# A graph network's edge step on one Trainium2 core: the destination-row products of the next group move from ahead of its source rows to right behind the current group's state products

## The chip, the core and the metric

The kernel runs on 1 core of a Trainium2 chip. The core's engines work side by side, each through its own queue of instructions in order: PE (TensorE) multiplies matrices, ACT (ScalarE) applies functions, DVE (VectorE) does elementwise work, POOL (GpSimd) here issues indirect DMAs that gather rows, SP (SyncE) issues all other DMAs. They meet through semaphores: an instruction increments one when it ends, another waits until it has a value. The metric is the device time of one execution in microseconds (us).

## The reference

Four rounds of message passing over 3125 nodes and 50,000 edges, sorted by destination. The state of a node has 128 numbers, that of an edge too.

```
edge_attr = swish(edge_attr_raw @ enc_W + enc_b)
for _ in range(4):
    e_in = concatenate([edge_attr, x[src], x[dst]])
    e_upd = layernorm(swish(e_in @ eW1 + eb1) @ eW2 + eb2) * eg + ebeta
    edge_attr = edge_attr + e_upd
    agg = segment_sum(edge_attr, dst)
    x = x + layernorm(swish(concatenate([x, agg]) @ nW1 + nb1) @ nW2 + nb2) * ng + nbeta
out = layernorm(x0 + x)
```

The hidden layer of an edge is a sum of three products: one of the edge's own state, one of its source node, one of its destination node. The kernel makes the two node products once a round for all nodes, as tables (`p_table` for sources, `q_table` for destinations), and only looks rows up per edge.

## The kernel before, in words

Each round (a *step*, `s` from 0 to 3) runs over 98 groups `g` of 512 edges (4 tiles of 128), and then over the nodes in 5 chunks, which also writes the tables for the next step. All of a step is written out flat, with no loop on the chip. On PE, `fast_pe` (line 1192) sets the order of a step, and the four parts that it calls are made by `pe_parts` (line 1088):

- `turn(g + 2)`, line 1103: 8 transposes that bring the edge state of the group after next into the form that its products need. It waits for the state's DMA (`st`) and for ACT's copy of the transposes before (`eT`).
- `hidden(g)`: three sets of products that add up in one PSUM tile `ps_h(g % 2)`. Line 1123: 4 *destination-row* products of 256 columns, which place the rows of `q_table` on edges by a 0/1 matrix; they wait for that window and matrix (semaphore `q`), and for DVE to have read the PSUM tile's last content (`hl` of group g - 2). Line 1131: 16 *source-row* products of 128 columns, which add the gathered rows of `p_table`; they wait for POOL's gathers (`rows`), and the last one signals `src`. Line 1139: 6 *state* products of 512 columns; they wait for `eT`, and signal `h`.
- `output(g - 1)`, lines 1150 and 1155: the second layer of the group before, a bias product and 24 products of 128 columns, into `ps_v`. It waits for `hl`, and signals `v`.
- `node_sums(g - 7)`, line 1171: 8 products that sum an older group's edges by destination. It signals `sum`.

So the order on PE was, for each g: rows of q (1123), source rows (1131), state (1139), transposes (1103), output (1150, 1155), sums (1171), then again with g + 1.

The other engines in a group: POOL issues 4 gathers (line 1080) for group g + 4 into the buffer that the source rows of g leave, so it waits for `src` of g. ACT makes swish of the hidden layer (lines 1242, 1243; waits for `h`), copies the transposes (1269), squares the output (1257; waits for `v`), and casts (1283). DVE makes the low half of the hidden layer (1349, signals `hl`), adds an older group's sum to `agg` (1419; waits for `sum`), finishes the norm (284 to 292, 1385, 1396, 1404), and reads the output (1359). SP issues the loads of group g + 3 (1022, 1030, 1036) and the loads and stores of older groups (1045, 1049).

The buffers for gathered rows are four deep, those for hidden and output PSUM two deep.

## Time and profile before

| what | value |
|---|---|
| median of 3 runs | 3248.82 us (3248.39 to 3252.28) |
| span of the profiled execution | 3309.1 us |
| PE busy | 2595.5 us, 78% |
| DVE busy | 2336.3 us, 71% |
| ACT busy | 2083.8 us, 63% |
| POOL busy | 1702.6 us, 51% |
| granted TensorE clock, mean | 0.947 |
| DMA | 578.05 MB, mean 175 GB/s |

The profile is of one execution, whose span from the first to the last instruction is 3309.1 us; what lies around that span isn't in it. That span is 60.3 us above the median of the runs, so a sum made on it is carried over as a ratio. "Busy" counts the time in which an engine has an instruction in work. A row of the timeline gives start, length, engine, line and operation, the tile written and the tile read, how many such instructions were merged (x16), and in brackets the engine's idle time ahead of it with what ended that. "issue" there means that the profile shows no wait, "remote" that it can't name who ended it.

### The profile page before, as it was taken

How to read it: one execution, taken by the hardware profiler on the slowest of the kernel's cores; microseconds unless marked ns; L12 is line 12 of the kernel's file. 1: busy time of each engine (PE TensorE's matmuls, PEld its weight loads, DVE VectorE, ACT ScalarE, POOL GpSimd, SP SyncE). 2: the span in 40 equal slices, each digit the busy share in tenths (PEclk: the TensorE clock that was granted, in tenths of full speed). 3: DMA queues.
4: the chain of work that ended last, by engine and by line, in shares of the span. 5: the costliest groups of instructions: out<-in, count | busy, mean ns of one | idle time of the engine just before them, and what ended most of it. 6: DMA issues, size and time to landing. Idle time of an engine off the chain costs nothing.

```text
span 3309.1 us, 86038 instructions
## 1 busy us (share of the span) xinstructions
PE 2595.5 (78%) x28086; PEld 1911.6 (58%) x28086; DVE 2336.3 (71%) x6778; ACT 2083.8 (63%) x5559; POOL 1702.6 (51%) x1679
## 2 busy tenths in 40 slices
PE   3665888888887788888887788888888688888886
PEld 1332666666664566666665566666665466666664
DVE  6884677777784577777786477777776377777777
ACT  3774666666663566666664566666675466666674
POOL 2445566566531556665640666665540665666550
PEclk8656999999999899999999899999999899999998
DMA  4776566666644566666653566666663455555550
GB/s 129 249 248 205 171 196 194 195 200 195 194 149 134 159 194 195 202 196 194 198 166 121 155 198 199 196 195 201 194 182 111 146 158 156 163 156 161 159 149 25
DMA packets 492918, 578.05 MB, mean 175 GB/s; under 512 B 82399, under 2 KB 341724, under 8 KB 492446
## 3 DMA queue, kind: packets, MB, share of 16 engines
q1 hardware_dynamic: 417198, 366.82, 34.8%
q0 software_dynamic: 75264, 205.62, 23.0%
q8 instruction: 228, 3.74, 0.5%
q14 instruction: 228, 1.87, 0.2%
HBM read 428.62 MB, written 144.35 MB: 173 GB/s over the span
## 4 chain that ended last, share of the span: by engine, by line
PE 59%; issue 16%; ACT 6%; DVE 6%; another core or an unknown queue 6%; DMA 3%; SPq 1%; DVEq 1%; POOL 0%; ACTq 0%; POOLq 0%
PE psum L1155 13%; PE psum L1139 13%; PE psum L1131 12%; PE psum L1123 5%; PE psum L1103 5%; PE psum L1171 4%; PE psum L1150 2%; PE psum L1577 2%; PE psum L1616 2%; ACT arena L1269 1%; ACT psum L1243 1%; ACT arena L1257 1%; PE psum L1590 1%; DMA arena<-attr_p 1%
## 5 line engine op out<-in xcount | busy, mean ns | idle before, releaser
L1080 POOL DMA_INDIRECT arena<-node_tables,idx_all x1568 | 1582.0, 1009 | 1342.0 <-PE psum L1131 626.5
L1257 ACT ACTIVATE arena<-psum 128x128 f32<-128x128 f32 x1568 | 411.6, 278 | 741.3 <-remote 723.1
L1131 PE MATMUL psum<-ident,arena 128*128 128x128 f16 x6272 | 548.1, 220 | 410.6 <-issue 398.8
L1131 PEld LDWEIGHTS psum<-ident,arena 128*128 128x128 f16 x6272 | 399.3, 98 | 541.1 <-issue 521.9
L1349 DVE SCALAR_TENSOR_TENSOR arena<-psum,arena 128x1024 f16<-128x1024 f32 x392 | 477.0, 1217 | 202.9 <-issue 146.9
L1155 PE MATMUL psum<-w_hi,arena 128*128 128x128 f16 x6272 | 595.2, 220 | 4.6 <-DVE arena L1349 3.5
L1155 PE MATMUL psum<-w_lo,arena 128*128 128x128 f16 x3136 | 550.5, 220 | 1.2 <-issue 1.2
L1419 DVE TENSOR_TENSOR agg<-agg,psum 128x128 f32 x392 | 113.0, 288 | 569.5 <-remote 544.8
L1242 ACT ACTIVATE arena<-psum 128x1024 f16<-128x1024 f32 x392 | 402.2, 1026 | 172.3 <-remote 75.7
L1155 PEld LDWEIGHTS psum<-w_hi,arena 128*128 128x128 f16 x6272 | 502.2, 98 | 6.8 <-DVE arena L1349 4.7
L1139 PE MATMUL psum<-arena,w_hi 128*128 128x512 f16 x1568 | 479.7, 386 | 29.8 <-issue 29.6
L1385 DVE SCALAR_TENSOR_TENSOR arena<-arena 128x128 f32<-128x128 f32 x1568 | 489.9, 346 | 4.0 <-DVE arena L288 0.4
L1269 ACT COPY arena<-psum 128x1024 f16<-128x1024 f16 x392 | 400.0, 1020 | 45.7 <-remote 22.0
L1243 ACT ACTIVATE psum<-psum 128x1024 f32<-128x1024 f32 x392 | 401.2, 1023 | 0.0
L1155 PEld LDWEIGHTS psum<-w_lo,arena 128*128 128x128 f16 x3136 | 308.8, 98 | 48.3 <-issue 3.5
L1257 ACT ACTIVATION_READ_ACCUMULATOR arena<-psum 128x1 f32 x1568 | 325.8, 208 | 0.0
L1139 PE MATMUL psum<-arena,w_lo 128*128 128x512 f16 x784 | 303.1, 387 | 7.8 <-issue 7.6
L1103 PEld LDWEIGHTS psum<-ident,arena 128*128 128x128 f16 x3136 | 211.5, 100 | 144.1 <-issue 46.6
L1359 DVE TENSOR_TENSOR arena<-psum,g_row 128x512 f32<-128x512 f32 x392 | 266.3, 679 | 30.3 <-ACT arena L1257 27.5
L1396 DVE SCALAR_TENSOR_TENSOR arena<-arena 128x512 f32<-128x512 f32 x392 | 279.2, 712 | 6.7
L1123 PE MATMUL psum<-arena 128*128 128x256 fp8e4 x1568 | 253.0, 274 | 36.3 <-issue 23.2
L1103 PE MATMUL psum<-ident,arena 128*128 128x128 f16 x3136 | 245.5, 222 | 41.4 <-DMA arena<-state 18.2
(172 smaller groups left out, 3514.9 us busy)
## 6 DMA issues: line engine op xcount, KB each, us to landing
state<-arena SPq DMA_DIRECT2D x392, 256.0 KB, 3.8
arena<-state SPq DMA_DIRECT2D x392, 256.0 KB
arena<-matrices SPq DMA_DIRECT2D x784, 64.0 KB
arena<-node_tables SPq DMA_DIRECT2D x784, 64.0 KB
node_tables<-arena SPq DMA_DIRECT2D x100, 256.0 KB, 2.4
arena<-node_tables,idx_all POOLq DMA_INDIRECT x1568
arena<-rel_rows SPq DMA_DIRECT2D x98, 128.0 KB, 3.9
matrices<-arena SPq DMA_DIRECT2D x98, 128.0 KB, 3.6
```

Of the source, the lines that this page charges most:

```text
L1080: pool.indirect_dma_start(out=rows[k][:, t, :], out_offset=None, in_=p_table, in_offset=bass.IndirectOffsetOnAxis(ap=idx_all[:, g, t:t + 1 ...
L1103: x = pe.transpose(ps_t[:, n * P:(n + 1) * P], st_in[k8][:, t, p * D:(p + 1) * D], ident16[:, :])
L1123: pe.matmul(ps_h(k2)[:, half, :].rearrange("q (t p) -> q t p", t=TPG)[:, :, h * HALF_N:(h + 1) * HALF_N], q_win[k][:, h * H + half * D:h * ...
L1131: x = pe.matmul(ps_h(k2)[:, half, t * P:(t + 1) * P], rows[k][:, t, p * H + half * D:p * H + half * D + D], ident16[:, :], start=False, st ...
L1139: x = pe.matmul(ps_h(k2)[:, half, :], w[:, cols], eT[k2][:, p, :], start=False, stop=w is w1_lo, skip_group_check=True)
L1155: x = pe.matmul(ps_v(k2)[:, t * P:(t + 1) * P], h[k2][:, half, t * P:(t + 1) * P], w[:, half, :], start=False, stop=half == 1 and h is hl, ...
L1242: act.activation(hh[k2], ps_h(k2), ACT.Silu).then_inc(S("hh"), 1)
L1243: act.activation(ps_h(k2), ps_h(k2), ACT.Silu).then_inc(S("h32"), 1)
L1257: x = act.activation(sq[k2][:, t * P:(t + 1) * P], ps_v(k2)[:, t * P:(t + 1) * P], ACT.Square, accum_out=nv[pair][:, n:n + 1])
L1269: act.copy(eT[k2].rearrange("p k e -> p (k e)"), ps_t[:, :]).then_inc(S("eT"), 1)
L1349: dve.scalar_tensor_tensor(hl[k2], ps_h(k2), 1.0, hh[k2], ALU.mult, ALU.subtract).then_inc(S("hl"), 1)
L1385: x = dve.scalar_tensor_tensor(e_new[k][:, t * P:(t + 1) * P], gu[k][:, t * P:(t + 1) * P], rs[pair][:, n:n + 1], st_in[k8][:, t, D:2 * D] ...
```

## The change

The 4 destination-row products of a group (line 1123, with their waits for `q` and `hl`) become a part of their own, `targets`. In a step's order it stands ahead of the loop for group 0, and in the loop right behind `hidden(g)` for group g + 1; before, it was the first piece of `hidden(g + 1)`, behind `node_sums(g - 7)`. No product is added, removed or changed, and no other engine's order is changed. The body of the general path (`pe`, for other inputs) keeps its order.

```diff
-                def hidden(i, off):
+                def targets(i, off):
                     if not self.has(i, off):
                         return
...
+                def hidden(i, off):
+
+                    if not self.has(i, off):
+                        return
+                    k, k2 = off % R, off % 2
                     pe.wait_ge(*self.gathered_dyn(s, i, off))
...
             def fast_pe(self, pe, s, node):
...
                 turn(0, 0)
                 turn(0, 1)
+                targets(0, 0)
                 for g in range(G1):
                     hidden(0, g)
+                    targets(0, g + 1)
                     turn(0, g + 2)
                     output(0, g - 1)
                     node_sums(0, g - LAG - 3)
```

The lines behind it shift by six: line 1131 is 1137 afterwards, 1139 is 1145, 1150 is 1156, 1155 is 1161, 1171 is 1177; 1103 and 1123 keep their numbers.

The order on PE in the middle of a step before, from the last output product of one group to the transposes of the next (the names in brackets are the semaphores waited for; `edge_oh` is the matrix of the sums, `edge_rows` the gathers, `edge_st` the state):

```order
L1155 MATMUL psum<-w_hi,arena 128x128
L1171 MATMUL psum<-arena 128x128 [waits edge_oh2,edge_el,edge_added]
L1171 MATMUL psum<-arena 128x128 x7
L1123 MATMUL psum<-arena 128x4x64 [waits edge_q2,edge_hl]
L1123 MATMUL psum<-arena 128x4x64 x3
L1131 MATMUL psum<-ident,arena 128x128 [waits edge_rows2]
L1131 MATMUL psum<-ident,arena 128x128 x15
L1139 MATMUL psum<-arena,w_hi 128x512 [waits edge_eT]
L1139 MATMUL psum<-arena,w_hi 128x512
L1139 MATMUL psum<-arena,w_lo 128x512
L1139 MATMUL psum<-arena,w_hi 128x512 x2
L1139 MATMUL psum<-arena,w_lo 128x512
```

The same stretch on PE now:

```order
L1161 MATMUL psum<-w_hi,arena 128x128
L1177 MATMUL psum<-arena 128x128 [waits edge_oh2,edge_el,edge_added]
L1177 MATMUL psum<-arena 128x128 x7
L1137 MATMUL psum<-ident,arena 128x128 [waits edge_rows2]
L1137 MATMUL psum<-ident,arena 128x128 x15
L1145 MATMUL psum<-arena,w_hi 128x512 [waits edge_eT]
L1145 MATMUL psum<-arena,w_hi 128x512
L1145 MATMUL psum<-arena,w_lo 128x512
L1145 MATMUL psum<-arena,w_hi 128x512 x2
L1145 MATMUL psum<-arena,w_lo 128x512
L1123 MATMUL psum<-arena 128x4x64 [waits edge_q3,edge_hl]
L1123 MATMUL psum<-arena 128x4x64 x3
```

The source rows now follow the sums directly, and the destination-row products of the group after stand behind the state products, ahead of the transposes, the output and the sums.

At the start of a step, on PE, the second group's place before:

```order
L1139 MATMUL psum<-arena,w_lo 128x512
L1103 MATMUL psum<-ident,arena 128x128 [waits edge_eT,edge_st2]
L1103 MATMUL psum<-ident,arena 128x128 x7
L1123 MATMUL psum<-arena 128x4x64 [waits edge_q1]
L1123 MATMUL psum<-arena 128x4x64 x3
L1131 MATMUL psum<-ident,arena 128x128 [waits edge_rows1]
```

And now:

```order
L1145 MATMUL psum<-arena,w_lo 128x512
L1123 MATMUL psum<-arena 128x4x64 [waits edge_q1]
L1123 MATMUL psum<-arena 128x4x64 x3
L1103 MATMUL psum<-ident,arena 128x128 [waits edge_eT,edge_st2]
L1103 MATMUL psum<-ident,arena 128x128 x7
L1137 MATMUL psum<-ident,arena 128x128 [waits edge_rows1]
```

There the wait for the second group's window (`edge_q1`) has moved ahead of the third group's transposes.

## Rows read from the trace of the kernel before

**Rows 1.** Waits over the whole span: who waited for whom, us in total, times, longest.

```profile
ACT arena L1257 <- remote: 723.1, 353, 3.2
POOL arena L1080 <- PE psum L1131: 626.5, 361, 3.6
...
PE psum L1131 <- issue: 398.8, 769, 1.9
```

**Rows 2.** Windows of two steps, gathers (line 1080) alone: us, POOL busy, (xcount).

```profile
409.00:935.00 526.00, 315.65 (x313) 1.00 0.67 197
...
2677.00:3180.00 503.00, 305.06 (x302) 1.00 0.55 158
```

**Rows 3.** The chain that ended last, 1500 to 1514 us: start, us, what.

```profile
1503.59 0.45 PE psum L1171 x8
1504.03 0.44 PE psum L1123 x4
```

**Rows 4.** Timeline of one group in mid-step: start, us, engine, line, count, [idle before].

```profile
1500.56 1.20 POOL L1080 DMA_INDIRECT arena<-node_tables,idx_all  x1 [1.94 <-PE psum L1131]
...
1503.31 0.95 POOL L1080 DMA_INDIRECT arena<-node_tables,idx_all  x1 [0.30 <-issue]
...
1503.37 0.22 PE L1155 MATMUL psum<-w_hi,arena 128*128 128x128 f16 x1
...
1504.31 0.33 PE L1131 MATMUL psum<-ident,arena 128*128 128x128 f16 x3
...
1504.92 0.33 PE L1131 MATMUL psum<-ident,arena 128*128 128x128 f16 x3 [0.28 <-issue]
...
1506.42 0.67 PE L1131 MATMUL psum<-ident,arena 128*128 128x128 f16 x9 [0.53 <-issue]
1506.54 0.28 ACT L1257 ACTIVATE arena<-psum 128x128 f32<-128x128 f32 x1 [2.04 <-remote]
...
1507.36 0.94 POOL L1080 DMA_INDIRECT arena<-node_tables,idx_all  x1 [1.85 <-PE psum L1131]
```

**Rows 5.** Timeline of a group whose output products end early against the gathers.

```profile
487.39 0.94 POOL L1080 DMA_INDIRECT arena<-node_tables,idx_all  x1 [1.06 <-PE psum L1131]
...
488.90 0.22 PE L1155 MATMUL psum<-w_hi,arena 128*128 128x128 f16 x1
...
489.84 0.74 PE L1131 MATMUL psum<-ident,arena 128*128 128x128 f16 x6
...
493.25 0.28 ACT L1257 ACTIVATE arena<-psum 128x128 f32<-128x128 f32 x1 [3.14 <-remote]
```

**Rows 6.** Timeline of a group whose output products end late against the gathers.

```profile
2186.05 0.22 PE L1155 MATMUL psum<-w_hi,arena 128*128 128x128 f16 x1
...
2186.99 0.83 PE L1131 MATMUL psum<-ident,arena 128*128 128x128 f16 x9
2188.20 0.55 PE L1131 MATMUL psum<-ident,arena 128*128 128x128 f16 x7 [0.38 <-issue]
```

**Rows 7.** Timeline of an early group of a step, which has no sums yet.

```profile
1875.19 0.22 PE L1155 MATMUL psum<-w_hi,arena 128*128 128x128 f16 x1
...
1875.68 0.94 PE L1131 MATMUL psum<-ident,arena 128*128 128x128 f16 x14
```

**Rows 8.** Timeline of two groups in a row, the first without a stop in its source rows.

```profile
1379.84 1.35 POOL L1080 DMA_INDIRECT arena<-node_tables,idx_all  x1 [1.63 <-PE psum L1131]
...
1383.58 1.06 PE L1131 MATMUL psum<-ident,arena 128*128 128x128 f16 x16
...
1386.32 0.94 POOL L1080 DMA_INDIRECT arena<-node_tables,idx_all  x1 [1.38 <-PE psum L1131]
...
1393.04 1.34 POOL L1080 DMA_INDIRECT arena<-node_tables,idx_all  x1 [1.55 <-PE psum L1131]
```

**Rows 9.** Timeline of the group of rows 4: DVE's low half, SP's window load.

```profile
1503.66 1.23 DVE L1349 SCALAR_TENSOR_TENSOR arena<-psum,arena 128x1024 f16<-128x1024 f32 x1 [0.27 <-issue]
...
1506.36 0.95 SPq L1036 DMA_DIRECT2D arena<-node_tables  x2
```

More of the change, by code:

```diff
@@ L1173, in node_sums @@
                     x.then_inc(S("sum"), 1)
-                return turn, hidden, output, node_sums
+                return turn, targets, hidden, output, node_sums
             def pe(self, pe, s):
-                turn, hidden, output, node_sums = self.pe_parts(pe, s)
+                turn, targets, hidden, output, node_sums = self.pe_parts(pe, s)
                 turn(0, self.lo)
@@ L1183, in body @@
                     for j in range(self.U):
+                        targets(i, j)
                         hidden(i, j)
@@ L1192, in fast_pe @@
             def fast_pe(self, pe, s, node):
-                turn, hidden, output, node_sums = self.pe_parts(pe, s)
+                turn, targets, hidden, output, node_sums = self.pe_parts(pe, s)
                 node_hidden, node_output, node_tables_of = node.pe_parts(pe, s)
```

## The prediction, made before the changed kernel ran

> **What bounds the kernel now.** I read the waits over the span first: who waits for whom, summed. Three stand out [rows 1]: ACT's square (line 1257) waits 353 times, 723 us, for an event the profile calls "remote"; POOL's gathers (1080) wait 361 times, 627 us, for the source rows (1131); and PE itself is idle 399 us ahead of source rows with "issue", which names no wait. There are 392 groups, so each happens nearly once a group. Next the windows over the gathers alone, which give the cycle: 313 gathers in 526.00 us are 6.72 us per four, 302 in 503.00 are 6.66 [rows 2]. PE's own work is less: in rows 4 it starts 7 rows between 1504.31 and 1506.42, 0.4 us of work in 2.1 us, so 1.7 us of a cycle are idle and 5.0 are work. PE's amount of work does not bound, whatever its share of busy time.
>
> The timeline of one group shows the ring [rows 4]. POOL starts its first gather at 1500.56. PE starts the last output product at 1503.37, goes through sums and targets (0.45 and 0.44 us in the chain, [rows 3]), starts source rows at 1504.31, and then stops: 3 rows, a gap, a few more, gaps of 0.28 and 0.53 us. At 1506.42 it runs free and does the last 9 rows. At 1506.54, within 0.12 us of that, ACT gets the signal `v` of the output product that had been started 3.17 us earlier, having idled 2.04 us. So products, and the signals of products already done, are held up together and come free together. What does the release follow? From the first gather to ACT's start it is 1506.54 - 1500.56 = 5.98 us here, and 493.25 - 487.39 = 5.86 where PE was early [rows 5], though from the last output product it is 3.17 against 4.35 us. The release keeps step with POOL's four gathers, not with PE. Behind it come the source rows that are left; the last signals `src`; and POOL's next first gather starts, 1507.36 here, 0.82 us behind the release.
>
> So a cycle is 5.9 us of gathers up to the release, then the rows left, then the signal. One row takes (1.06 - 0.22) / 15 = 0.056 us, from a run of 16 and the 0.22 us that one product alone shows [rows 4, 8]. Nine rows left put 8 x 0.056 = 0.45 us on the path. The floor is seen where all 16 rows were done before the release: 1386.32 - 1379.84 = 6.48 us, and the cycle behind it took 6.72 again, a mean of 6.60 for the pair [rows 8]. Only the rows left at the release can be bought, up to 6.70 - 6.48 = 0.22 us a group (6.70 the rounded mean of rows 2).
>
> **What decides how many are left.** PE stops 1.1 us after its last output product: 8 sums, 4 targets and 3 rows got started (1503.37 to 1504.47, [rows 4]). In the early group it is 8, 4 and 6, up to about 490.2 [rows 5]; in the late group 8, 4 and 9 [rows 6]. Where there are no sums, 4 targets and 14 rows got through [rows 7]. The count behind `v` is thus 15, 18, 21, and 18: it does not depend on what kinds the products are, and the group without sums has simply brought more source rows through. I read this as an allowance behind the held signal: PE may start some 15 to 21 products past `v`.
>
> **The change part by part.** It adds and removes no instruction. It takes 4 targets, 0.44 us, out of the stretch between `v` and the source rows and puts them behind the state products, ahead of transposes and output.
> - Source rows relative to `v`: 0.44 us, or 4 products, closer. With the same allowance 4 more rows start before the stop: 9 left become 5. Saved 4 x 0.056 = 0.22 us at most per group, which lands on the floor (6.48).
> - `v` itself: 0.44 us later against the source rows ahead of it. Its natural end would still be well ahead of the release: in rows 4 it is held by more than 2 us (ACT's idle time). So this costs nothing in the held groups. Cover gone, it is 0.44 us in a group.
> - `hl` wait moved ahead: targets for g + 1 need DVE's low half of g - 1. DVE ends it at 1503.66 + 1.23 = 1504.89 [rows 9]; the moved targets start behind the state products, which come behind the last row, so after 1506.42 + 8 x 0.056 = 1506.9. Margin over 2 us. Behind them on PE stand transposes, output and sums; none waits. Cost 0.
> - `q` wait moved ahead past transposes, output and sums (at most half a cycle, 3.4 us). SP loads at 1506.36 a window that is for a later group [rows 9], about three ahead: a cycle of 6.7 us or more is left. Cost 0. No DMA and no queue of SP or POOL is moved.
> - At a step's start the second group's window is now waited for ahead of the third group's transposes, 8 products of 128 columns like the rows (8 x 0.056 = 0.45 us) that no longer cover the wait: at most 4 x 0.45 = 1.8 us, at least 0. Near the end, where no gathers run, `v` comes 0.44 us later; with some four such groups a step that is 0 to 7 us in all. I take 1 us for both, since PE is ahead of the others there, and do not carry it into the sum.
>
> How much of the 0.22 us stays is the unknown. If every group is brought to the floor it is 0.22; if groups alternate as in rows 8, each short one followed by a long one, the mean is 6.60 and the gain 0.10. Less than zero is bounded by the rival below (+0.22). I take 0.12, near the alternating pair, the only row that shows a short cycle and what follows it. Groups: 353 waits of ACT [rows 1] are 88 a step; less the first eight of a step, without sums and mostly through their rows already [rows 7], 80 x 4 = 320. Sum: 320 x 0.12 = 38 us, 3309.1 - 38.4 = 3270.7 us of profiled span. As a ratio that is 0.9884, and on the median of 3248.82 it gives 3211 us. All of the 0.22 would be 70 us, ratio 0.9787, 3180 us; 0.10 gives 3217 us.
>
> **Rivals.**
> *No change, 3249 us.* The profiled span is 60.3 us above the median. Over 320 groups that is 0.19 us a group, close to the 0.22 us above the floor. If the drip of rows exists only in the profiled execution, timed runs already cycle at POOL's 6.48 and nothing is to be had; the profile after would be shorter and the runs not. For it: the size agrees, and POOL never shows a cycle under the floor. Against it: without any hold the cycle would be near PE's 5.0 us and the runs far shorter than 3249, so most of the hold is in them. The same result comes if the release follows the last rows rather than POOL, or if POOL's 0.5 us from signal to gather grows. The Trainium skill, page "NOTIFIC — the notification-queue block", section "7.1 Overflow: three behaviours, one of which stalls the engine", says that the path from engine to queue never drops a record but backpressures, so recording can hold up an engine. No row here tells a record from a signal; by that rule the profiled stops would be those of the recorder, and the time would be this rival's.
>
> *Slower, about 3318 us.* The stop may be set not by a count behind `v` but by the time since a gather began: in rows 4 the third gather starts at 1503.31 and PE stops 1.16 us later. If PE may start only so many products after that moment, the targets, which take 0.11 us each where rows take 0.056, no longer carry it through that time; source rows start 0.44 us sooner against PE's own order, but PE's whole phase is set by `src`, so the output products come 0.44 us later after it, and with them everything behind. Then the rows reached at the stop do not rise, and by the count lost, 4 rows more are left: 0.22 us x 320 = 70 us, span 3379.5, 3318 us. It decides where the moment of the third gather falls within output or sums. Against it: in rows 6 nine rows were started with the same four targets, and in rows 5 six, at another phase to the gathers; and rows 7 show count, not phase. For it: the phase between source rows and gathers is by construction nearly fixed, so the three rows do not vary it much.
>
> *Moved waits, 3250 to 3258 us.* The step's start and end cost their 1.8 and 7 us and the gain in the middle is nil.
>
> **How the numbers follow.** The forecast has 0.44 (all faster outcomes, from 3165 to 3242), no change 0.34, the slow rival 0.16, moved waits 0.06. A measurement of this kernel tells about 0.2%, 6.5 us, from no change. The likeliest gives 3211 us, its own range 3180 to 3240. The range of eight in ten takes in the unchanged case and the moved waits: 3180 to 3268. Left out is the full slow rival and what would be beyond the floor.
>
> **What the profile after would show.** Right: windows over line 1080 give 6.5 to 6.6 us per four gathers in place of 6.7; behind ACT's start at 1257 run 4 to 5 rows, not 9; PE's stop begins some 15 to 18 products after the last output product with 7 or more rows done; POOL's wait for the source rows falls by 0.1 us a gather set. Wrong: the same windows at 6.7 with as many rows left, meaning the stop is not counted from `v`; or 6.9 and more, with 12 to 13 left. A wait of PE at line 1123 of over 0.3 us in mid-step would mean that the moved `q` or `hl` wait has no margin. A shorter span with unchanged runs would speak for the first rival.

## The result, and the profile after

The changed kernel took 3257.46 us (median of 20 runs, 3251.22 to 3261.22), the kernel before 3252.07 us in the same series (median of 20, 3243.91 to 3262.22). The ratio is 1.0015, with a 95% interval of 1.0008 to 1.0022: no gain, if anything a trace slower. The forecast was 3211 us. Ratios compare executions in the faster of two states; two executions fell out of it, one of the kernel before at 7612 us and one of two_targets at 3361 us, both on chip 12.

The profiled execution of the changed kernel has a span of 3254.9 us, 2 us under its own time of 3256.65. That of the kernel before had 3309.1 us, while the slowest of its 20 runs took 3262.22 us, so the profile is of none of them. This matters for all that compares the two profiles below. The waits of the changed kernel over the whole span, in us in total, times, longest:

```profile
ACT arena L1266 <- remote: 655.9, 347, 3.2
POOL arena L1080 <- PE psum L1137: 530.8, 354, 3.7
...
PE psum L1137 <- issue: 326.2, 699, 2.7
```

These answer to [rows 1]. All three fell, by 67, 96 and 73 us. The gathers over the window of the same 526 us as in [rows 2], and over the last step (us, POOL's busy time, number of gathers):

```profile
409.00:935.00 526.00, 335.53 (x321) 0.99 0.68 202
2677.00:3180.00 503.00, 304.25 (x296) 0.99 0.55 158
```

321 in place of 313 gathers in 526 us is a cycle of 6.55 us in place of 6.72. (The second window holds 296 in place of 302: the changed kernel's last step ends 54 us earlier, and the window reaches into its tail.) Seen against [rows 4], a pair of groups shows what the forecast had in mind. Start, us, engine, line, count, idle time before:

```profile
802.86 1.43 POOL L1080 DMA_INDIRECT arena<-node_tables,idx_all  x1 [1.35 <-PE psum L1137]
...
805.85 0.94 POOL L1080 DMA_INDIRECT arena<-node_tables,idx_all  x1 [0.30 <-issue]
...
806.10 0.22 PE L1161 MATMUL psum<-w_hi,arena 128*128 128x128 f16 x1
...
806.61 1.08 PE L1137 MATMUL psum<-ident,arena 128*128 128x128 f16 x14
...
808.07 0.27 PE L1137 MATMUL psum<-ident,arena 128*128 128x128 f16 x2 [0.38 <-issue]
...
808.91 0.28 ACT L1266 ACTIVATE arena<-psum 128x128 f32<-128x128 f32 x1 [2.11 <-remote]
...
809.40 0.95 POOL L1080 DMA_INDIRECT arena<-node_tables,idx_all  x1 [1.35 <-PE psum L1137]
...
812.01 1.39 POOL L1080 DMA_INDIRECT arena<-node_tables,idx_all  x1 [0.30 <-issue]
...
812.49 0.22 PE L1161 MATMUL psum<-w_hi,arena 128*128 128x128 f16 x1
...
812.99 0.28 PE L1137 MATMUL psum<-ident,arena 128*128 128x128 f16 x2
...
813.72 0.38 PE L1137 MATMUL psum<-ident,arena 128*128 128x128 f16 x4 [0.45 <-issue]
...
814.46 0.45 PE L1137 MATMUL psum<-ident,arena 128*128 128x128 f16 x5 [0.35 <-issue]
...
815.20 0.44 PE L1137 MATMUL psum<-ident,arena 128*128 128x128 f16 x5 [0.30 <-issue]
...
815.34 0.28 ACT L1266 ACTIVATE arena<-psum 128x128 f32<-128x128 f32 x1 [2.00 <-remote]
...
815.92 1.47 POOL L1080 DMA_INDIRECT arena<-node_tables,idx_all  x1 [1.26 <-PE psum L1137]
```

The source rows now start 0.5 us behind the last output product (806.10 to 806.61), where it was 0.94 [rows 4]. But it is the output product that has moved, not the rows. From POOL's first gather to the last output product it is 806.10 - 802.86 = 3.24 us, where it was 1503.37 - 1500.56 = 2.81; from the first gather to the first source row it is 806.61 - 802.86 = 3.75 us, and it was 1504.31 - 1500.56 = 3.75. In the first group all 16 are started by 808.13, 0.8 us ahead of the release at 808.91. But POOL does not start then. It starts at 809.40, 0.49 us behind the *release*: the signal `src` is held like every other. From first gather to first gather this is 6.54 us, near the 6.48 of [rows 8]. In the next group the source rows meet the stop after 2 products, and the last 5 come with the release; its cycle is 6.52 us.

By profile against profile this looked like a success: 54 us less, where the sum had said 38. By the runs it was nothing: either the profile of before was not typical, or the change is worth less than it seems. The experiments were to tell these apart.

In what follows the same quantities were counted from each timeline over the 332 groups from the 9th to the 91st of each step. The release is taken as ACT's start on `v`. "Left" is the number of source rows that start later than 0.14 us ahead of it, since the last burst of rows begins by about that much before ACT does (1506.42 against 1506.54 in [rows 4]). "The first stop" is the first pause of over 0.33 us between the starts of two products behind the last output product.

### The profile page after: what moved, and what is told of

It is laid out like the page before. It is cut to its first block, busy times and chain, and to the rows that moved or that the text cites. A ratio compares the mean times of both kernels' runs of the same rounds, so it can differ in the third digit from the quotient of the medians.

```text
span 3254.9 us, 86038 instructions
## 1 busy us (share of the span) xinstructions
PE 2596.9 (80%) x28086; PEld 1917.8 (59%) x28086; DVE 2347.8 (72%) x6778; ACT 2081.9 (64%) x5559; POOL 1735.2 (53%) x1679
## 3 DMA queue, kind: packets, MB, share of 16 engines
q8 instruction: 228, 3.74, 0.5%
## 4 chain that ended last, share of the span: by engine, by line
PE 71%; issue 14%; DVE 5%; DMA 3%; another core or an unknown queue 3%; ACT 2%; SPq 1%; DVEq 1%; POOL 0%; ACTq 0%; POOLq 0%
PE psum L1145 16%; PE psum L1161 15%; PE psum L1137 14%; PE psum L1177 5%; PE psum L1103 5%; PE psum L1123 5%; PE psum L1156 3%; PE psum L1586 2%; DMA arena<-attr_p 2%; PE psum L1625 2%; PE psum L1599 1%; PE psum L784 1%; DVE arena L1394 1%; DVEq L885 0%
## 5 line engine op out<-in xcount | busy, mean ns | idle before, releaser
L1080 POOL DMA_INDIRECT arena<-node_tables,idx_all x1568 | 1613.4, 1029 | 1252.3 <-PE psum L1137 530.8
L1137 PE MATMUL psum<-ident,arena 128*128 128x128 f16 x6272 | 542.3, 220 | 336.3 <-issue 326.2
L1137 PEld LDWEIGHTS psum<-ident,arena 128*128 128x128 f16 x6272 | 386.6, 98 | 449.5 <-issue 435.8
L1145 PE MATMUL psum<-arena,w_hi 128*128 128x512 f16 x1568 | 488.0, 390 | 36.2 <-issue 35.5
L1177 PE MATMUL psum<-arena 128*128 128x128 fp8e4 x3136 | 248.2, 219 | 26.8 <-issue 21.1
L1413 DVE SCALAR_TENSOR_TENSOR arena<-arena 128x512 f16<-128x512 f32 x392 | 268.6, 685 | 0.2
L1123 PE MATMUL psum<-arena 128*128 128x256 fp8e4 x1568 | 245.1, 279 | 29.3 <-issue 16.5
```

The costliest lines, as they stand in the source:

```text
L1080: pool.indirect_dma_start(out=rows[k][:, t, :], out_offset=None, in_=p_table, in_offset=bass.IndirectOffsetOnAxis(ap=idx_all[:, g, t:t + 1 ...
L1123: pe.matmul(ps_h(k2)[:, half, :].rearrange("q (t p) -> q t p", t=TPG)[:, :, h * HALF_N:(h + 1) * HALF_N], q_win[k][:, h * H + half * D:h * ...
L1137: x = pe.matmul(ps_h(k2)[:, half, t * P:(t + 1) * P], rows[k][:, t, p * H + half * D:p * H + half * D + D], ident16[:, :], start=False, st ...
L1145: x = pe.matmul(ps_h(k2)[:, half, :], w[:, cols], eT[k2][:, p, :], start=False, stop=w is w1_lo, skip_group_check=True)
L1177: x = pe.matmul(ps_a[:, 0:P], st_out[k][:, t, p * D:(p + 1) * D], oh[k][:, t * P:(t + 1) * P], start=t == 0 and p == 0, stop=t == TPG - 1 ...
```

## The experiments

Six series were run, and they fall into levels. "Held" means that recorded updates of semaphores, of engines and transfers alike, grow rare from about 3 us behind POOL's first gather on (1 to 3 in each half us up to 5.5 us), and then come in a burst (12 to 20 in each half us up to 6.5; before, before_3, after, after_3). In before_again they come evenly, 14 to 18 in each half us. A series ran on one chip each, so a property of the chip can't be told from one of the series.

| series | before, median us | held |
|---|---|---|
| chip 14 | 2734 | no |
| chip 4 | 2728 | no |
| the case's own | 3252 | yes |
| chip 5 | 3259 | yes |
| chip 12 | 3308 | yes |
| chip 2 | 3309 | yes |

### Both kernels again (before_again, after_again, before_2, before_3, after_3)

No edit. What was expected of before_again:

> The kernel before, unchanged, for a second profile. What is to be told apart: the first profile of before has a span of 3309 us, 60 above its median, and a steady cycle of 6.71 us; the changed kernel's has 3255, equal to its median, and 6.56. Theory A: the first profile was an unusual execution of before; the usual one has a span near 3250, a mean steady cycle near 6.55 us and 5 or 6 source rows left at the release, so that nothing was there to be bought. Theory B: the profile of before is always some 60 us longer than the runs; then it comes out near 3309 again with 8 rows left. Ratio to before 1.000 +- 0.001.

Of after_again:

> The changed kernel again. Theory A: ratio 1.000 to 1.003, span and median within 3 us of each other, steady cycle 6.55 us as in its first profile. Theory B gives the same. If its profile now comes out at 3309 while its runs stay at 3257, both spans are possible for both kernels.

Measured on chip 14: before_again 2734.87 us, ratio 0.9994 (0.9982 to 1.0007); after_again 2729.40 us, ratio 0.9982 (0.9971 to 0.9994). Neither theory had this: the whole kernel takes 16% less there. The changed kernel is 5 us faster on that chip. The timeline of the kernel before on chip 14:

```profile
1009.68 0.38 PE L1150 MATMUL psum<-v_bias,ones 128*128 128x512 f16 x1
...
1012.04 0.95 POOL L1080 DMA_INDIRECT arena<-node_tables,idx_all  x1 [0.30 <-issue]
...
1012.12 1.06 PE L1131 MATMUL psum<-ident,arena 128*128 128x128 f16 x16
...
1012.20 0.29 ACT L1257 ACTIVATE arena<-psum 128x128 f32<-128x128 f32 x1
...
1013.29 0.95 POOL L1080 DMA_INDIRECT arena<-node_tables,idx_all  x1 [0.30 <-issue]
...
1014.75 0.38 PE L1150 MATMUL psum<-v_bias,ones 128*128 128x512 f16 x1
```

No stop in the 16 source rows, and no "remote" wait of ACT. From output to output it is 5.07 us: PE is packed here, and POOL gathers without rest, one each 1.25 us. (The mean of all groups counted is 5.29 us.) The stops and waits on which the prediction stood are not there.

> The kernel before once more. The first series ran with every semaphore update held between 2.5 and 5.3 us behind POOL's first gather (cycle 6.5 to 6.7 us, 3250 us in all); the second, on a chip numbered 14, ran the same kernels without the hold (cycle 5.07 us, 2734 us). Theory H: the hold is a property of the chip or the execution, not of the kernel; so this comes out either near 2734 or near 3250, with nothing between. If it is near 3250: theory A says its profile shows a mean steady cycle near 6.55 us and 5 or 6 rows left at the release; theory B says 6.7 us and 8 rows with a span 60 us above the median.

On chip 4: 2725.36 us, ratio 0.9998 (0.9978 to 1.0018). Not held either.

> The kernel before on whatever chip comes. Chips 14 and 4 ran it without held updates (2734 and 2728 us), the series of the case with them (3252 us). Theory H: one of the two states again, nothing between. Near 3250 it gives the missing second profile of before with held updates: mean steady cycle near 6.55 us (theory A) or near 6.7 us (theory B).

On chip 12: 3310.16 us, ratio 1.0008 (0.9995 to 1.0020), span 3301.7. This is a second profile of before with held updates, and it reads like the first: cycle 6.70 us, 7.0 rows left (the first: 6.72 and 7.9), and its waits are near those of [rows 1]:

```profile
ACT arena L1257 <- remote: 736.4, 361, 3.2
POOL arena L1080 <- PE psum L1131: 604.8, 359, 3.9
...
PE psum L1131 <- issue: 380.3, 754, 3.7
```

But on this chip the runs too are at 3308, and this profiled execution is one of them. So B falls. The first profile of before reads like an ordinary execution at the 3308 level, beside runs at the 3252 level; that it was taken on another chip is likely and not shown. Whether theory A's 6.55 us and 5 or 6 rows hold for the kernel before at the 3252 level stays open, since no profile of it was taken there.

> The changed kernel beside the kernel before on one chip more. So far three levels of before were seen: 2731 (chips 14, 4; no held updates), 3252 (the case's series) and 3308 (chip 12, held, where before's profile read like the one of rows 1 to 9: span 3302, cycle 6.69). Held updates: theory G (given back: fewer rows are left at the release, but POOL then starts late in the next group, so the mean stays near the floor of the hold) expects a ratio of 0.997 to 1.002, as targets_late had 0.997; the prediction's sum expects 0.988. Not held: 0.998.

On chip 5: 3260.76 us, ratio 1.0004 (0.9994 to 1.0013), cycle 6.58 us, 5.5 rows left. The ratio is as theory G had it; its reason is tested under targets_late. The profile of the changed kernel on chip 5 is like its first one; its time equals that of the kernel before on the same chip.

### Targets behind the transposes (targets_late)

```diff
-                    targets(0, g + 1)
                     turn(0, g + 2)
+                    targets(0, g + 1)
```

> The changed kernel with the targets of g + 1 behind the transposes of g + 2, ahead of the output. Without held updates, theory W (what the change gains there, 5 us, comes from the 0.44 us of targets that stand ahead of the transposes and cover their wait for SP's load of the state, whose sum fell from 107 to 46 us): the gain is gone, the transposes wait about 107 us again, ratio to before 0.999 to 1.001. Rival W2, the gain comes from the targets' leaving the stretch ahead of the source rows: it stays, 0.997 to 0.999. With held updates: as the changed kernel, 1.000 to 1.003, by either.

On chip 12 (held): 3299.15 us, ratio 0.9970 (0.9958 to 0.9981). For the stretch between output and source rows this is the same edit as the change, and it has the kernel before's profile beside it on the same chip. Gathers in two windows, first before_3, then targets_late:

```profile
1150.00:1650.00 500.00, 302.16 (x298) 1.00 0.67 197
2650.00:3150.00 500.00, 311.71 (x301) 1.00 0.56 160
```

```profile
1150.00:1650.00 500.00, 312.64 (x300) 0.99 0.67 198
2650.00:3150.00 500.00, 315.37 (x302) 1.00 0.56 160
```

599 against 602 gathers in 1000 us: 6.68 and 6.65 us a cycle, 0.03 us or a quarter of what the forecast took. The runs, 9.2 us faster, say 0.02 us a group. Three things were counted to see why it is so little.

First, the place of PE's work against POOL's gathers (medians, us behind POOL's first gather; the stop behind the third):

| | last output product | first source row | first stop, behind the third gather | products from the last output product to the stop |
|---|---|---|---|---|
| before | 2.81 | 3.74 | 1.20 | 15 |
| before_3 | 2.81 | 3.74 | 1.21 | 14 |
| targets_late | 3.24 | 3.74 | 1.19 | 11 |
| after | 3.24 | 3.74 | 1.17 | 11 |
| after_3 | 3.24 | 3.75 | 1.18 | 11 |

The change moves the output product 0.43 us later. The source rows start where they did, since PE's work from one group's rows to the next is the same in sum. The stop stays where it was too, against the gathers, and the products that pass behind `v` fall from 14 or 15 to 11. An allowance counted from `v` would have kept its number. Within each of these kernels it is the same: a later output product doesn't move the stop (slope -0.07 to -0.32, where a count would give 1).

Second, the parts of the cycle (means, us):

| | last row to POOL's start | POOL's start to release | release to last row | cycle | left | groups with none left |
|---|---|---|---|---|---|---|
| before_3 | 0.617 | 5.937 | 0.143 | 6.697 | 7.0 | 28 |
| targets_late | 0.772 | 5.952 | -0.046 | 6.678 | 5.7 | 62 |

The last row comes 0.19 us sooner against the release, but this is a mean in which groups that are through before the release count as negative. What stands on the path is only what runs behind the release, and that shrinks from 0.245 to 0.195 us. The first column grows for the same reason: in groups with no row left POOL starts 1.72 us behind the last row in targets_late, against 0.55 in the others, because it starts with the release.

Third, the cycle of before_3 by rows left: 6.52 us with none to 3, 6.61 with 4 to 7, 6.78 with 8 to 11. So below 4 rows nothing more is gained. At these prices the rows left in targets_late would be worth 0.05 us; measured are 0.02, since its groups with 4 to 11 left take 0.03 to 0.05 us longer than those of before_3. Theory G's reason, a long group behind each short one, is hardly there: behind a group with none left the cycle is 6.72 us in targets_late and 6.67 behind the others, which makes under 0.01 us in the mean, and in after and after_3 it is not longer at all (6.55 against 6.57, 6.57 against 6.58). One such group and the one behind it, in targets_late, a case where it was long:

```profile
841.74 1.39 POOL L1080 DMA_INDIRECT arena<-node_tables,idx_all  x1 [1.50 <-PE psum L1137]
...
845.49 1.09 PE L1137 MATMUL psum<-ident,arena 128*128 128x128 f16 x15
...
846.97 0.22 PE L1137 MATMUL psum<-ident,arena 128*128 128x128 f16 x1 [0.39 <-issue]
...
847.75 0.28 ACT L1266 ACTIVATE arena<-psum 128x128 f32<-128x128 f32 x1 [2.06 <-remote]
...
848.24 0.94 POOL L1080 DMA_INDIRECT arena<-node_tables,idx_all  x1 [1.34 <-PE psum L1137]
...
853.34 0.38 PE L1137 MATMUL psum<-ident,arena 128*128 128x128 f16 x4 [0.46 <-issue]
...
854.09 0.83 PE L1137 MATMUL psum<-ident,arena 128*128 128x128 f16 x12 [0.37 <-issue]
...
854.30 0.28 ACT L1266 ACTIVATE arena<-psum 128x128 f32<-128x128 f32 x1 [2.12 <-remote]
```

PE was through at 846.97, 0.78 us ahead of the release; POOL came at 848.24 all the same, and the group behind it had 10 rows left and started its next gathers only at 855.19.

### Half the targets (two_targets)

```diff
-                            for h in range(2):
+                            for h in range(2 if off < 2 and s == 0 else 1):
```

> The changed kernel with 2 of the 4 targets of every group but the first two left out (half the destination rows are missing). Without held updates, theory P (PE is packed, 5.07 us a group is its own work): 0.22 us x 390 = 86 us less, ratio 0.967. Rival, POOL's gathers at 4 x 1.25 = 5.0 us a group are the floor: ratio over 0.985. With held updates: no change by either, since PE is not the bound there, ratio 0.99 to 1.00.

On chip 12: 3287.32 us, ratio 0.9932 (0.9914 to 0.9951). This run starts from the changed kernel, so it is to be held against targets_late on the same chip: 0.22 us of PE work less a group, 86 us in all, gave 12 us (21 against before). So where updates are held PE's amount of work is mostly, not wholly, off the path.

### Sums ahead of the output too (sums_ahead, sums_ahead_2, sums_ahead_3)

```diff
-                    output(0, g - 1)
                     node_sums(0, g - LAG - 3)
+                    output(0, g - 1)
```

> The changed kernel with the node sums ahead of the output products too, so that the source rows follow the output directly, 0.45 us nearer to its signal. Theory 1 (gathers set a floor of about 6.45 us, and after already is within 0.1 us of it): no gain, 3240 to 3262 us, though rows left at the release fall from 5 to 1 or 2. Rival, the rows left are still what costs: 4 fewer of them give 0.2 us a group, 3190 us.

> The changed kernel with the sums ahead of the output. Where updates are held: theory A (after is within 0.1 us a group of a floor that the held updates set) gives ratio 0.995 to 1.003; the prediction's theory (4 more products off the stretch are 0.2 us a group) gives 0.98. Where they are not held: 0.995 as in the series before.

> Sums ahead of the output too. Held updates: theory G 0.995 to 1.002, with half the groups or more at 0 rows left; the prediction's mechanism, doubled, 0.976. Not held: 0.995 to 0.997, as twice before.

Measured: chip 14, 0.9949 (0.9930 to 0.9968); chip 4, 0.9971 (0.9956 to 0.9987); chip 5 (held), 0.9984 (0.9975 to 0.9993). On chip 5 it stands beside after_3:

| | last row to POOL's start | POOL's start to release | release to last row | cycle | left | groups with none left |
|---|---|---|---|---|---|---|
| after_3 | 0.699 | 5.882 | -0.004 | 6.578 | 5.5 | 64 |
| sums_ahead_3 | 1.009 | 5.889 | -0.331 | 6.567 | 3.8 | 113 |

1.7 rows fewer are left (0.09 us at 0.056 a row). The last row comes 0.33 us sooner against the release, POOL's start behind it comes 0.31 us later, and the cycle falls by 0.01. Within one chip and one series this says that fewer rows left at the release buy next to nothing here. extra_ops below says it too: 3.8 rows left, cycle 6.58. It is the best of the kernels that keep the order of the gathers, by 0.2 to 0.5% against before.

### Fewer gathers (half_gathers, half_gathers_2, half_gathers_3, three_gathers)

```diff
-                    for t in range(TPG):
+                    for t in range(2):
                         pool.indirect_dma_start(
...
-                                              rows[k][:, t, ...
+                                              rows[k][:, t % 2, ...
```

and the counts waited for with 2 in place of 4; three_gathers has 3.

> The changed kernel with 2 gathers for a group in place of 4; the source rows use each gathered tile twice (this part of the computation is changed). Theory 1, the gathers of POOL and the release behind them set the cycle (5.9 us from first gather to release, of 4 gathers): the release comes some 2.5 us sooner, PE's own 5.0 us bound, cycle 6.56 to about 5.1, time down by 1.4 x 340 = 480 us to about 2780. Rival, PE's stops have another source (its own signals, or SP's loads and stores) and POOL only follows: cycle still over 6.3 us, time over 3160.

> The changed kernel with 2 gathers for a group in place of 4 (source rows use each gathered tile twice, which changes that part of the computation). Where updates are held (before near 3250): if the hold follows the gathers, the cycle falls to about 5.1 us and the time to about 2800; if it has another source the time stays over 3150. Where they are not: 2645 us as in the series before, ratio 0.967.

> 2 gathers for a group in place of 4 (source rows use each tile twice). Held updates: if the hold comes from the gathers' work or their updates (32 of some 220 a group fewer), the cycle falls to 5.1 to 5.9 us, time under 3050; if the hold has nothing to do with them, over 3200. Not held: 2646 as before.

> The changed kernel with 3 gathers for a group in place of 4 (the fourth tile's source rows use the first's). Held updates: theory T (there is a threshold in how densely gathers come; with 3 in 5.07 us POOL rests 1.3 us and the hold goes) expects 5.1 to 5.3 us a group and a ratio of 0.82 to 0.84, as with 2. Rival R2 (each gather costs a fixed part of the hold, 1.6 us): 4.9 us, so PE's 5.07 again or a little over; rival K2, one hold for each group that ends with its last gather's landing, 1.3 us sooner: cycle 5.3 to 5.5 us, ratio 0.84 to 0.87. Not held: 0.967 to 0.975.

Not held: 0.9665 (0.9643 to 0.9686) on chip 14, 0.9706 (0.9679 to 0.9733) on chip 4. Held: 0.8191 (0.8173 to 0.8209) on chip 5, 2669 us in place of 3259. The gathers are what makes the hold; with 2 a held chip is no slower than another by more than 1%. (Their number, their bytes and POOL's time in them fall together here, and no run tells these apart.) The timeline on chip 5 with 2 gathers:

```profile
1204.22 1.01 POOL L1080 DMA_INDIRECT arena<-node_tables,idx_all  x1 [2.55 <-PE psum L1137]
...
1205.53 0.95 POOL L1080 DMA_INDIRECT arena<-node_tables,idx_all  x1 [0.30 <-issue]
...
1207.96 1.06 PE L1137 MATMUL psum<-ident,arena 128*128 128x128 f16 x16
...
1208.05 0.29 ACT L1266 ACTIVATE arena<-psum 128x128 f32<-128x128 f32 x1
...
1209.29 0.99 POOL L1080 DMA_INDIRECT arena<-node_tables,idx_all  x1 [2.81 <-PE psum L1137]
```

POOL's start comes each 5.07 us, all 16 rows pass, ACT does not wait. With three gathers, on chip 2: 0.8629 (0.8613 to 0.8644), 2857 us. Windows of 400 us on chip 2 (three) and chip 5 (two):

```profile
1000.00:1400.00 400.00, 224.03 (x215) 1.00 0.73 212
```

```profile
1000.00:1400.00 400.00, 163.33 (x150) 1.00 0.70 204
```

The first is 400 / (215 / 3) = 5.6 us a group. So held chips take 5.1, 5.6 and 6.6 us with two, three and four gathers. That is nearest to rival K2, one hold a group that ends behind the last gather: its ratio is met (0.84 to 0.87), its cycle missed by 0.1 us. That the hold ends with the last gather's landing is not shown by this.

### The gathers spread (spread_gathers)

```diff
                     for t in range(TPG):
+                        if t == 2 and g - R - 1 >= self.lo:
+                            pool.wait_ge(S("v"), s * self.per_step + g - R)
                         pool.indirect_dma_start(
```

> The changed kernel, all work kept, with POOL waiting for v of two groups back ahead of the third of a group's four gathers. With held updates (before 3250 to 3310): theory Q (the hold comes where a third and fourth gather follow the first two with no pause; half_gathers on such a chip had none) expects the hold to go and the cycle to fall from 6.58 us to what POOL then needs, about 0.5 + 2.5 + 0.8 + 2.5 - 0.7 = 5.6 us: 380 us less, ratio 0.88. Rival K, it is the number of gathers in a cycle and not their spacing: the hold stays, third gathers now wait for the held v, cycle 6.6 to 8 us, ratio 1.00 to 1.15. Without held updates: a cycle of 5.6 for 5.27 us, ratio 1.03 to 1.05.

On chip 2 (held): 3220.23 us against 3309.45, ratio 0.9733 (0.9717 to 0.9749). All of the work is kept. The hold did not go, so theory Q falls; nor did the cycle grow, as rival K had it. It is the fastest full kernel seen on a held chip. One of its windows (309 gathers is 6.47 us a group):

```profile
1150.00:1650.00 500.00, 299.81 (x309) 1.00 0.69 204
```

The cycle is even: of its groups, from the 10th to the 90th in a hundred, it lies between 6.43 and 6.52 us, where the changed kernel's first profile has 6.37 to 6.82. The number is near the 6.48 us of [rows 8], but the ring is another one. POOL's gathers now come in pairs, 3.2 to 3.3 us from pair to pair:

```profile
1481.08 1.03 POOL L1082 DMA_INDIRECT arena<-node_tables,idx_all  x1 [0.94 <-remote]
...
1482.42 0.94 POOL L1082 DMA_INDIRECT arena<-node_tables,idx_all  x1 [0.32 <-issue]
...
1484.14 0.28 ACT L1268 ACTIVATE arena<-psum 128x128 f32<-128x128 f32 x1 [0.34 <-remote]
...
1484.37 0.94 POOL L1082 DMA_INDIRECT arena<-node_tables,idx_all  x1 [1.00 <-remote]
```

ACT waits only 0.34 us for `v`, 7.3 rows are still left at the release, and POOL's first gather starts 3.18 us behind the last row. So it gained 0.23 us a group while the rows left stayed as many as in before_3: it does not show that the rows left were worth the 0.22 us. It took a pause of POOL, not an order of PE. On a chip that is not held it was not run; there POOL has no time to give, and the expectation of 1.03 to 1.05 stands untested.

### Transfers and records (thin_store, one_window, extra_ops)

thin_store:

```diff
-                    sp.dma_start(state[g, :, :], st_out[g % R]...
+                    sp.dma_start(state[g, 0:32, :], st_out[g % R]...[0:32, :])
```

> The changed kernel with SP's state store cut to 32 of 128 partitions (so later steps read old states in the others): a quarter of the packets, 50 MB less of 144 written. Where updates are held: if the amount of DMA traffic and of its updates makes the hold, time falls by over 3%; if only the gathers do, by less than 1%. Where they are not held: the pair of state load and store does not bound, ratio 0.99 to 1.00.

It came to chip 4, not held: 0.9948 (0.9925 to 0.9970), so it says nothing of the hold. But the traces do: in the last step no state is stored, and 160 GB/s move in place of 197 in before_3's two windows above, at nearly the same number of gathers (301 for 298). The mean cycle of the last step is 6.65 us, of the other three 6.71.

one_window loads one window in place of two (`for h in range(1)` in `load_rows`, both halves of the targets read it):

> The changed kernel with one of the two window loads of a group left out (both halves of the targets use the first): one SP transfer fewer of nine transfers beside the four gathers, 64 KB of 1470. Held updates: theory Q or T, the gathers alone make the hold: ratio 0.99 to 1.00. Rival U (the hold is a queue of all transfers' updates, each of a fixed time): 16 of some 150 fewer, cycle 10% shorter, ratio 0.91. Not held: 0.99 to 1.00.

On chip 2: 0.9898 (0.9882 to 0.9915). A queue of all transfers' updates would have given 0.91. Its cycle is 6.62 us on the mean of the steps.

extra_ops:

```diff
+                    for m in range(16):
+                        dve.memset(scrap[:, m:m + 1], 0.0)
                     dve.wait_ge(S("sum"), c(i, off))
```

> The changed kernel with 16 tiny operations more on DVE in each group (a memset of one column, 128x1), put where DVE waits for the sums (1.6 us a group with held updates), so that they fill idle time and take nothing from PE or POOL. Held updates: theory R (what holds the updates is the recording of instructions and updates, so a cycle is as long as its records: 199 instructions and some 80 to 170 recorded updates a group, now 16 more) expects 4 to 6% of the cycle, 120 to 190 us more; theory N (the hold is a matter of transfers) expects under 10 us. Not held: DVE is 85% busy, 0 to 1% more by both.

On chip 5: 3268.88 us, ratio 1.0036 (1.0021 to 1.0051), 8 us above after_3, within theory N's 10 us and far from 120. So the number of recorded instructions does not set the hold. The Trainium skill, page "NOTIFIC — the notification-queue block", section "7.1 Overflow: three behaviours, one of which stalls the engine", says that the path of records backpressures inside rather than dropping one; a price per instruction record, as that could have meant here, is refuted by this run, but the records of updates and of transfers were not varied by themselves, and every execution here has a recorded span and clock, so none is known to be without records. The records differ, too: landings of transfers are 60 to 65 a group in the traces of before, before_3, after and after_3, and 147 in before_again and after_again, for the same kernels. Held traces thus lack half of the updates, which the page's rule would not lead one to expect; whether what loses them also holds the signals is untested. With 2 gathers it is 65 on chip 5 against 120 on chip 14 at the same cycle of 5.12 us, so records can be missing without the hold.

## Why the prediction was wrong

Point by point, by its own steps.

- **The ring of held signals** was read rightly. `v` and `src` come with a release about 5.9 us behind POOL's first gather, and half_gathers_3 shows that the gathers make it: with two of them 590 us go.
- **"With the same allowance 4 more rows start before the stop: 9 left become 5."** This step failed, and with it the mechanism. The stop is not counted from `v`. It keeps to POOL's gathers (1.20 and 1.21 us behind the third before, 1.17 to 1.19 after), and so do the source rows (3.74 us behind the first gather, before and after). What moved is the output product, 0.43 us later. So the products past `v` fell from 14 or 15 to 11, and rows left fell not by 4 but from 7.0 to 5.7 on chip 12. (From 7.9 to 5.2 between the two first profiles, which are of different levels.) That 15, 18, 21 and 18 products had passed in four groups was read as a count; by all groups it goes by timing. Why 1.3 rows fewer are left at all, with start and stop where they were, stays open.
- **"Saved 4 x 0.056 = 0.22 us at most per group", and of it "I take 0.12".** Mis-sized. The work behind the release shrank by 0.05 us on chip 12, and the cycle by 0.02 (0.03 by the windows). In the runs of the changed kernel nothing came of it (1.0015 and 1.0004 on two chips). Groups with none to 3 rows left have the same cycle (6.52 us in before_3), so a row is not worth 0.056 us there.
- **Only the rows left can be bought, down to 6.48 us.** Not borne out as a bound. In after and after_3 groups with none left take 6.45 us on the mean, and single cycles are as short as 6.29; in targets_late, on chip 12, 6.54. And spread_gathers took 89 us (0.23 us a group over 392) with 7.3 rows left.
- **The base of the sum.** 3309.1 us of span was carried to 3248.82 as a ratio. Those are two levels, 3309 and 3252. At the level of the runs the changed kernel shows a cycle of 6.56 to 6.58, while the kernel before's there has not been seen; by equal times on chip 5 it should be near 6.58 too, which is an inference and no profile. So of the 6.70 from which the sum started, 0.12 us may not have been there in the runs at all.
- **Moved waits** cost nothing that shows. PE's wait for the first windows of a step is 12.2 us in three waits on chip 14 against 11.3, and 12.7 and 10.9 on held chips against 11.2. From a step's last group to the next step's first, by POOL's first gathers, it is 110.4 us in before and 110.2 in after, 109.7 in before_3 and in after_3. The measured 3257 us lies within this rival's 3250 to 3258, but that is luck.
- **The slower rival** had the right cause and the wrong consequence. It said that the stop goes by the gathers and that the output products come 0.44 us later, and both are so. But it priced this at 4 rows more left. Since the source rows start at the same moment against the gathers, about as many of them have passed at the first stop as before (4.7 on the mean in before_3, 5.7 in targets_late), and the cost is nil.
- **The first rival** was right in its number, 3249. Of its reasons, a hold that is only in the profiled execution falls: the profiled executions of after and before_3 are among the timed runs. The 60 us between profile and runs were a sign of another level, as in chips 12 and 2. That the records of updates have a part in the hold of all runs is not excluded.

The stated range, 3180 to 3268 us, held the result only through its unchanged case. Open is what the hold is, why series differ in it (none, 3252, 3309), what in the gathers sets the moment of the stop, and how the kernel before cycles at the 3252 level. On the chips that are not held the change gains 0.18%. PE's weight loads wait 107 us for the state there before, and 46 after, since the targets stand ahead of the transposes; that they cover that wait was argued (theory W) and not tested, since targets_late came to a held chip. Putting the sums ahead of the output as well gave 0.3 to 0.5% against before on these chips.

## What to carry to other kernels

When a piece of work moves within one engine's order, draw both ends against the clock of the engine that sets the cycle: here the source rows came 0.44 us nearer to the output product because the output product came later, and against POOL nothing was won. A stop seen in four groups fits a count and a time equally well; all groups of the trace, plotted against either, tell them apart before anything is built. A profile whose span differs from the runs by more than their spread (here 1.9% against 0.1%) may be of another state of the machine: do not carry a sum over as a ratio before it is known which groups differ.

## What the runs showed of the hardware

- The same program took 2728, 2734, 3252, 3259, 3308 and 3309 us in six series, each with a spread under 0.7% (the one execution of 7612 us left out). The mean TensorE clock granted was 0.947 to 0.952 in the four profiles of it, two held and two not, so it is not the clock.
- On held chips the cycle was 5.1, 5.6 and 6.6 us for 2, 3 and 4 gathers of 128 rows; on chip 14 it was 5.12 us with 2 and 5.25 with 4 (the changed kernel).
- On held chips PE first stops 1.2 us behind POOL's third gather in the median, whether the last output product started 2.81 or 3.24 us behind the first gather; 14 and 11 products had passed by then (before_3, targets_late). After that it starts a few products each 0.74 us (812.99, 813.72, 814.46, 815.20 in the timeline of after).
- Traces of held chips have 60 to 65 landings of transfers a group, those of chip 14 have 147, for the same kernels (before_3, after_3; before_again, after_again).
- 16 memsets of one column on DVE added 8 us over 392 groups where DVE was idle.
